# Last linear weight blocks in two pairs of PSUM banks, the last expert's result rows stored by halves, and another order in the linear layer's first tile

## The reference

```python
# second block: mixture of 8 experts, each row goes to its best 2, with capacity
h = relu(einsum('ecd,edh->ech', disp, w1) + b1);  out = einsum('ech,ehd->ecd', h, w2) + b2
gathered = out[idx_k, loc_c]                       # per row, the 2 result rows
y = einsum('tk,tkd->td', gates_k * valid, gathered)
x = x + y
# third block: layernorm, linear layer, normalised sum over graph neighbours
h = layernorm(x) @ W.T + b
out = segment_sum(norm[:, None] * h[col], row);    x = x + out
# fourth block: layernorm, quantised feed-forward 1024 -> 4096 -> 1024
```

## Time and profile before

| | us |
|---|---|
| median of 3 runs | 1021.59 |
| profiled execution, its own time | 1022.45 |
| span in its trace | 1020.7 |
| PE busy in the span | 957.4 (94%) |
| VectorE busy | 758.3 (74%) |
| ScalarE busy | 432.4 (42%) |
| GpSimd busy | 211.0 (21%) |

### The profile page before, as it was taken

How to read it: one execution, slowest core, us unless ns; L and a number is a source line. 1 busy time by engine, 2 the same in 40 slices (tenths; PEclk the granted TensorE clock), 3 DMA queues, 4 the chain that set the end, 5 groups by cost and what they waited for, 6 DMA issues and landing times.

```text
span 1020.7 us, 17357 instructions
## 1 busy us (share of the span) xinstructions
PE 957.4 (94%) x6685; PEld 528.4 (52%) x6685; DVE 758.3 (74%) x1095; ACT 432.4 (42%) x541; POOL 211.0 (21%) x203
## 2 busy tenths in 40 slices
PE   1799889999699999999979999999999999999998
PEld 0688745554466655555644434455544444444443
DVE  6999878786766666655778974587769768796874
ACT  5354435563255666655552211477634221222400
POOL 6300034221220001110033310010139990000000
PEclk9999899999699999999989999999999999999999
DMA  3900025554798888997645868499820555555672
GB/s 105 270 2 2 2 77 200 220 206 151 244 343 313 311 312 316 333 342 273 238 138 169 202 162 205 173 374 352 298 42 21 124 124 104 117 129 131 138 140 83
DMA packets 174850, 191.04 MB, mean 187 GB/s; under 512 B 135193, under 2 KB 135515, under 8 KB 170687
## 3 DMA queue, kind: packets, MB, share of 16 engines
q1 hardware_dynamic: 168383, 167.57, 52.5%
q0 software_dynamic: 6400, 22.55, 7.0%
HBM read 137.98 MB, written 36.38 MB: 171 GB/s over the span
## 4 chain that ended last, share of the span: by engine, by line
PE 87%; DVE 7%; issue 3%; DMA 1%; ACT 1%; DVEq 0%; POOL 0%; SPq 0%; ACTq 0%
PE ps L1167 20%; PE ps L1363 14%; PE ps L1436 9%; PE ps L1274 9%; PE ps L1345 8%; PE ps L1290 8%; PE ps L1387 3%; PE ps L1231 2%; PE ps L1023 1%; PE ps L1131 1%; DVE w1l L2211 1%; PE ps L1096 1%; PE ps L1041 1%; PE ps L1050 1%; DMA abs_e<-in_L_ffn_w 1%
## 5 line engine op out<-in xcount | busy, mean ns | idle before, releaser
L1363 PE MATMUL ps<-w1q,xqt 128*128 128x512 fp8e4 x640 | 139.3, 379 | 0.7 <-issue 0.7
L1753 ACT ACTIVATE hf<-ps,fs 128x512 f32<-128x512 f32 x80 | 54.9, 687 | 142.0 <-PE ps L1363 142.0
L1363 PEld LDWEIGHTS ps<-w1q,xqt 128*128 128x128 f16 x640 | 62.5, 98 | 76.0 <-issue 1.2
L870 POOL TENSOR_TENSOR rstd<-mv,consts 128x1 f32<-128x1 f32 (+1 forms) x40 | 29.0, 733 | 317.7 <-DVE mv L1880 230.1
L1167 PE MATMUL ps<-gwt_h,xt 128*128 128x512 f16 x320 | 84.6, 379 | 0.9 <-issue 0.9
L1167 PE MATMUL ps<-wt_h,xt 128*128 128x512 f16 x320 | 85.4, 379 | 0.0
L1274 PE MATMUL ps<-xdh,w1h 128*128 128x314 f16 x256 | 76.3, 298 | 3.0 <-DVE w1l L2211 2.7
L2461 DVE TENSOR_REDUCE hm<-hf 128x1 f32<-128x512 f32 x80 | 51.6, 680 | 35.3 <-ACT hf L1753 35.1
L1274 PE MATMUL ps<-xdh,w1l 128*128 128x314 f16 x256 | 75.8, 296 | 0.0
L1274 PE MATMUL ps<-xdl,w1h 128*128 128x314 f16 x256 | 75.6, 295 | 0.0
L1345 PE MATMUL ps<-hs_h,at_h 128*128 128x512 f16 x200 | 59.5, 379 | 0.8 <-DVE hs_l L2429 0.8
(11 more groups left out here) (342 smaller groups left out, 2120.0 us busy)
## 6 DMA issues: line engine op xcount, KB each, us to landing
wstage<-in_L_ffn_w SPq DMA_DIRECT2D x32, 1024.0 KB, 7.0
abs_in<-in_L_ffn_w SPq DMA_DIRECT2D x18, 1024.0 KB, 6.6
abs_e<-in_L_ffn_w SPq DMA_DIRECT2D x14, 1024.0 KB, 5.2
fnat_b<-in_L_ffn_w SPq DMA_DIRECT2D x28, 512.0 KB, 8.0
fnat_a<-in_L_ffn_w SPq DMA_DIRECT2D x27, 512.0 KB, 6.3
hq_d<-hq SPq DMA_DIRECT2D x18, 512.0 KB, 4.8
eo_d<-eo SPq DMA_DIRECT2D x16, 512.0 KB, 3.0
xs_d<-xs_all SPq DMA_DIRECT2D x10, 512.0 KB, 2.9
```

Source lines behind the costliest of these rows:

```text
L870: g.tensor_tensor(rstd[:, one], mv[:, one, 1], consts[:, 1:2], ALU.pow).then_inc(s_rstd, 1)
L1363: last = mm(ps[:, n % 4, :], xqt[:, u, k, :], w1q[:, k // 2, n * 512:(n + 1) * 512, k % 2], start=(k == 0), stop=(k == KD - 1))
L1753: cp(hf[:, i % 2, n * 512:(n + 1) * 512], ps[:, n % 4, :], ACT.Gelu, scale=fs[:, i % 2, 3:4]).then_inc(s_ge, 1)
```

## The change

It has six parts. (1) Blocks 5 and 7 of the linear weights are turned into banks 0 and 1 instead of 4 and 5, so that blocks 5, 6 and 7 wait only for the copies of the block before the one before; block 5 waits for the last eviction of expert results, which frees banks 0 to 2. (2) All three pieces of `ranked` come behind block 7. (3) SP issues the two transfers of the first half of the last rows when that half is evicted, for every expert. (4) On POOL `rstd` of tile i comes behind the gathers n = 2i+4 and 2i+5 instead of ahead of them. (5) In VectorE's list, `norm` of tile 0 comes ahead of the first addition of tile 1, and `low` and `copy_low` of tile 0 ahead of the second. (6) PE does 4 instead of 8 filling matmuls ahead of the first transposes, and the transposes of tile 1 stand ahead of depth 5 of product 0 instead of depth 3.

```diff
+        BLOCK_BANKS = (4, 4, 4, 4, 4, 0, 4, 0)
@@ SP, expert
-                    sp.wait_ge(s_g2r, 3 + 6 * e + 2 * s + 2)
+                    sp.wait_ge(s_g2r, 3 + 6 * e + 2 * s + (2 if s < 2 else 1))
...
                         sp.dma_start(rest[:, 0:512], eo[48:SM[s], u, 0:512]).then_inc(s_eoh[u], 16)
+                        sp.wait_ge(s_g2r, 3 + 6 * e + 2 * s + 2)
                         sp.dma_start(rows[:, 512:D], eo[64:64 + 48, u, 512:D]).then_inc(s_eoh[u], 16)
@@ POOL, gathers
-                if n % 2 == 1 and n >= 3:
-                    rstd_tile(2 * NT + n // 2 - 1, n // 2 - 1)
+                if n % 2 == 1 and n >= 5:
+                    rstd_tile(2 * NT + n // 2 - 2, n // 2 - 2)
+            rstd_tile(3 * NT - 2, NT - 2)
             rstd_tile(3 * NT - 1, NT - 1)
@@ PE, product
-                    if k == 3 and n not in (R_LIN1 - 1, R_LIN1 + NT - 1) and not by_transfer(n + 1):
+                    if k == (5 if n == R_LIN1 else 3) and n not in (R_LIN1 - 1, R_LIN1 + NT - 1) and not by_transfer(n + 1):
@@ PE, w1_t
-                pe.wait_ge(s_wth, i + 1)
+                pe.wait_ge(s_wth, i + 1 if i < 5 else i)
+                if i == 5:
+                    pe.wait_ge(s_g2r, 3 + 6 * NE)
...
-                    tr(bank16(4)[:, k * P:(k + 1) * P], gnh[:, u, k * P:(k + 1) * P], id16[:, :])
+                    tr(bank16(BLOCK_BANKS[i])[:, k * P:(k + 1) * P], gnh[:, u, k * P:(k + 1) * P], id16[:, :])
@@ PE, expert, the last one
                         w1_t(i)
-                        if i < KD - 1:
-                            ranked(i - 4, (6, 7, 3)[i - 4])
+                    for h, bank in enumerate((6, 7, 3)):
+                        ranked(h, bank)
@@ PE, ahead of the linear layer
-            kept_busy(8)
+            kept_busy(4)
@@ VectorE
             mixed_statistics(0)
+            norm(R_LIN1, 0, 0)
             mixed(1, 0)
-            norm(R_LIN1, 0, 0)
+            low(R_LIN1, 0)
+            copy_low(R_LIN1, 0)
             mixed(1, 1)
-            low(R_LIN1, 0)
             mixed_statistics(1)
-            copy_low(R_LIN1, 0)
             norm(R_LIN1, 1, 1)
```

More of the change, by code:

```diff
@@ L1237, in w1_t @@
                 pe.wait_ge(s_gnh, i + 1)
-                pe.wait_ge(s_wth, i + 1)
+                pe.wait_ge(s_wth, i + 1 if i < 5 else i)
+                if i == 5:
+                    pe.wait_ge(s_g2r, 3 + 6 * NE)
                 for k in range(KD):
-                    tr(bank16(4)[:, k * P:(k + 1) * P], gnh[:, u, k * P:(k + 1) * P], id16[:, :])
+                    tr(bank16(BLOCK_BANKS[i])[:, k * P:(k + 1) * P], gnh[:, u, k * P:(k + 1) * P], id16[:, :])
                 pe.wait_ge(s_gnl, 2 + i + 1)
-                pe.wait_ge(s_wtl, i + 1)
+                pe.wait_ge(s_wtl, i + 1 if i < 5 else i)
                 for k in range(KD):
-                    last = tr(bank16(5)[:, k * P:(k + 1) * P], gnl[:, u, k * P:(k + 1) * P], id16[:, :])
+                    last = tr(bank16(BLOCK_BANKS[i] + 1)[:, k * P:(k + 1) * P], gnl[:, u, k * P:(k + 1) * P], id16[:, :])
                 last.then_inc(s_wtp, 1)
@@ L1653, in w1_part @@
                 act.wait_ge(s_wtp, 2 + i + 1)
-                cp(gwt_h[:, :, i * P:(i + 1) * P], bank16(4).rearrange("p (k c) -> p k c", k=KD), ACT.Copy).then_inc(s_wth, 1)
+                cp(gwt_h[:, :, i * P:(i + 1) * P], bank16(BLOCK_BANKS[i]).rearrange("p (k c) -> p k c", k=KD), ACT.Copy).then_inc(s_wth, 1)
             def expert(e, ep):
@@ L2242, in w1_part @@
                 dve.wait_ge(s_wtp, 2 + i + 1)
-                v.tensor_copy(gwt_l[:, :, i * P:(i + 1) * P], bank16(5).rearrange("p (k c) -> p k c", k=KD)).then_inc(s_wtl, 1)
+                v.tensor_copy(gwt_l[:, :, i * P:(i + 1) * P], bank16(BLOCK_BANKS[i] + 1).rearrange("p (k c) -> p k c", k=KD)).then_inc(s_wtl, 1)
             def ranks():
```

## The result

The changed kernel is slower: 1025.63 us (median of 13 runs, 1023.09 to 1027.64) against 1021.84 us (13 runs) for the kernel before beside it, a ratio of 1.0034 with a 95% interval of 1.0025 to 1.0044. So the change costs 2.5 to 3.5 us, and the forecast of no change (1021.4, range to 1023.4) was wrong.

The account below looks back on a forecast made before the run. PE, busy 94% of the span and 87% of the chain, was taken as the bound. At product 2: +0.9 order, -1.5 earlier tile 0, +0.2 GpSimd, +0.2 clock = -0.2 us, giving 1021.4 us, range 1019.3 to 1023.4.

Parts of the forecast that it names:

- product 2 counts and not product 0: Linear layer's start: the end depends on when product 2 can start, since VectorE follows PE at 1 us behind product 0.
- the new order: VectorE's list in the first tiles: norm and low of tile 1 1.9 us later, product 2 0.9 us later.
- E: Seam between experts and linear layer: the end of the second addition of tile 0, 529.1 us in the trace before.
- The slack of `copy_low` at product 2: Copy of tile 2's low half before product 2: ready at 560.1, only 1.0 us ahead of PE at 561.1.
- The stores went out earlier: Last expert's stores on SP: the fourth issued 0.76 us sooner, so the data of tile 0 come sooner.
- g: Gain at the seam from the second addition of tile 0 ending sooner: 0.75 to 2.5 us, taken as 1.5.
- the clock, +0.2: First transposes with fewer filling matmuls: a half clock costs 0 to 1.3 us, taken as 0.2.
- the second rival: Transposes of tile 0: clock falls to 0.50, copy up to 1.3 us later, 1022.7 to 1023.5 us; chance 0.20.
- GpSimd's +0.2: rstd of tile 2 behind two gathers: starts 0 to 0.4 us later, taken as 0.2.
- behind it PE has no long wait until the end: Behind product 2: PE has no long wait until the end, so product 2's start sets the end.
- The store by halves in the other seven experts costs nothing: SP's stores in the seven other experts: no cost, as nothing anybody waits for is queued there in that 0.4 us.

Follow-up runs that it names:

- after_halves_last: The changed kernel with the stores by halves in the last expert alone; ratio 1.0035 to the kernel before.
- after_fill8: The changed kernel with stores by halves in the last expert only and 8 filling matmuls instead of 4; 1024.46 us, ratio 1.0013 to the kernel before.
- pool_only: The kernel before with only GpSimd's rstd of the linear layer's tiles put behind two gathers more; ratio 0.9995.
- delay_08: The kernel before with one more VectorE operation (about 0.9 us) ahead of norm of tile 1 of the linear layer; ratio 0.9998.
- halves_all: The kernel before with only the stores by halves, for all experts; ratio 1.0008.
- blocks_early_old_order: The changed kernel with VectorE's order, GpSimd's rstd, transpose depth and 8 filling matmuls as before, stores by halves in the last expert only; ratio 0.9992 to the kernel before.
- order_low_first: The kernel before with VectorE's new first-tile order and, from tile 2 on, low of the next tile ahead of the addition of the tile behind it; ratio 1.0048.
- after_copy_first: The changed kernel, halves in the last expert only, with copy_low of tile 2 and low of tile 3 ahead of the addition of tile 4; 1033.94 us, ratio 1.0110.

## Why the prediction was wrong

**Right:** product 2 counts and not product 0, and the new order puts VectorE's list 1.8 us later (1.9 on record) and product 2 0.9 later (after_halves_last and after_fill8: E + 32.8 for the 32.9 on record). The slack of `copy_low` at product 2 was 0.9 us and not 1.0, since PE's own start was at E + 31.86 (560.97) and not at 561.1. rstd fell from 1.55 to 0.57 us as soon as VectorE waited beside it. The stores went out earlier and the second addition waited for a DMA; g was 1.2 in the profile of the change, and 1.0 to 1.25 in all others with the early blocks, for the 1.5 taken.

**Mis-sized: the clock, +0.2 for a term of +1.3.** I had priced the low clock right (1.3 us at most) and judged it unlikely. Six of seven executions with four matmuls and the early blocks lost it; in the change's own two product 2 was then at E + 34.10 and not 32.8. That was the second rival, and its place and its size held: the granted clock fell within 532 to 533, behind thin work of PE. GpSimd's +0.2 did not appear (pool_only: copy of tile 2 at E + 30.14, 30.22 before). The Trainium skill, "TensorE: Matmul & The Clock Gate", Part 1, had it on this side too: the throttled clock is the default and activity releases it; the granted clock of 0.50 to 0.69 in six of seven executions agrees.

**The step that failed: "behind it PE has no long wait until the end".** It was read off the trace of before, where it was true only by a margin. I followed the list of VectorE to `copy_low` of tile 2 and stopped. Next to it in the same list stands `low` of tile 3, whose rows leave by DMA. The trace of before has the margin, in SP's queue and in the time from issue to landing of the two transposing transfers:

```profile
559.93 0.80 SPq L703 DMA_DIRECT2D xt_d<-xl  x1
563.62 2.32 SPq L713 DMA_TRANSPOSE xt<-xt_d  x1
...
573.91 4.11 SPq L713 DMA_TRANSPOSE xt<-xt_d  x1
```

```profile
DMA to landing us min/median/max: 6.2/6.2/6.2
```

```profile
DMA to landing us min/median/max: 7.5/7.5/7.5
```

The rows of tile 3 landed at 569.8 (E + 40.7), 1.5 us ahead of product 3 at E + 42.2, and those of tile 4 at 581.4 (E + 52.3), only 0.4 ahead of product 4 at E + 52.7. In the changed kernel the rows of tile 3 leave at E + 33.5 instead of E + 30.4 (1.8 from the list, 1.3 from the clock) and take 5.6 us to be written instead of 3.6 and 5.9 to come back instead of 6.2, while PE wants them 2.2 us later, with product 2. That makes 3.1 + 2.0 - 0.3 - 2.2 - 1.5 = 1.1 us of waiting, as in the trace. In delay_08 the list was 0.85 us late and product 2 was not, so a margin of 0.4 leaves 0.45 us of waiting at product 4; the trace has 0.50. I had not looked for the price that a transfer pays for traffic beside it: part 4 moves gathers beside that writing (pool_only alone: 5.75 us). With this the sum for the change reads 0.9 + 1.3 (clock) - 1.2 (g) = +1.0 at product 2, and +2.1 at product 3; the trace ends 2.0 later.

**"The store by halves in the other seven experts costs nothing"** is neither shown nor refuted. With the new order the kernels with and without it are alike (1.0034 and 1.0024 against 1.0035); with the old one they differ by 0.8 us (halves_all against 1) and 1.5 us (1.0006 against 0.9992 and 0.9990), within the intervals, and both profiles with it caught a transfer of 14 us at product 5. **Open as well** is the rest: the medians say 2.5 to 3.5 us for the change where the two traces of it show 2.0, and 3.6 for after_halves_last where its one trace shows 1.2. The turned rows land differently from execution to execution, so a single profile may miss some of it; that was not shown, nor that all of it lies in the seam.

**A version that beats the changed kernel:** the early blocks with the old order stood at 1021.54 and 1021.78 us, ratios 0.9992 and 0.9990. Both intervals lie below those of the changed kernel. Against the kernel before neither interval excludes 1, though both traces show the end 0.9 and 1.3 us nearer to the fixed point, which is about what g is (1.1 and 1.2).

## What to carry to other kernels

When a change delays an engine's list, follow that list past the next consumer, through every item that leaves by another way (a queue, a round trip through memory), and write down the slack of each; the free slack of the first one (0.9 us here) says nothing of the second (1.5 us for the rows of tile 3, 0.4 for those of tile 4). A transfer's duration read in the trace of before holds only for the company that it had there, so ask at what moment other queues will now start. And a gain ahead of a rigid list is worth only what the list itself moves: in the traces the early blocks brought about 1 us because they moved E, while a product 0 that started 2 us sooner behind E (after_halves_last) brought none.

## What the runs showed of the hardware

- A transposing transfer of 512 KB took 4.3 to 4.9 us from issue to landing in about half of the cases, most of them with no gather near, and 5.2 to 8.5 us in nearly all others (9.5 in one). It took 13.8, 14.0 and 14.3 us in the three cases in which it was issued 0.2 to 0.3 us behind the start of the second of two full gathers (1.5 to 2.5 us behind the first). With gathers of an eighth of the bytes at that distance it took 4.6 to 4.9. In blocks_early_old_order one was issued 0.04 us ahead of the second gather and took 7.8. Why so small a step doubles it is not known.
- The granted clock fell from 1.00 to 0.50 after an idle time of PE of 3.1 us in the middle of the products (order_low_first) and after 8.1 us (after_copy_first); that made one product 1.7 us longer and 24 matmuls 2.3 us longer (7.64 instead of 5.35). A wait is thus dearer than its length.
- GpSimd's gathers took 0.93 to 0.99 us to issue in most places. They took 1.7 to 1.98 us in some, and each of these had begun beside an operation of VectorE with two operands in SBUF (an addition or a low half); rstd was longer in the same way (1.55 against 0.57). Some lay between (1.06 to 1.52).
